# Expert tiles: transposition of bf16 halves by DMA in place of f32 transpositions on TensorE

## The chip, the cores and the metric

One core of one Trainium2 chip. The metric is the device time of one execution in microseconds.

## What is computed

A two-layer block on x of 32 x 256 x 256 (f32). Layer 0 is cross attention and then a mixture of experts; layer 1 is gated cross attention and then a quantized feed-forward network with a convolution. The change lies in the experts alone:

```
xf = layernorm(x).reshape(8192, 256)
scores = softmax(xf @ w_router.T);  weights, indices = top_k(scores, 2)
h = silu(xf @ w1[e]) * (xf @ w3[e])          # e = 0..7, hidden width 352
y = h @ w2[e]
out = sum over the two chosen experts of weight * y
```

The products are made as sums of bf16 products of high and low halves, three to each f32 product: high x high, high x low, low x high.

## The kernel before, in words

The program runs four stages in a row: `attention_first` (which also routes each token row to its expert's block of `sent_rows` in HBM), `experts`, `attention_second`, `ternary_ffn`. In the profiled execution `experts` lies at about 573 to 1050 us.

`experts` (line 1756) works on 71 tiles of 256 rows (NT = 2 blocks of 128 rows, D = 256 columns, KC = 2 chunks of 128 columns), each belonging to one expert. Every engine walks the list of tiles with its own instructions, written out; semaphores tie them together.

- SP: `load(b)` (L1860) brings a tile's rows into `xe`, one of four buffers, after the results of tile b - 4 were made (y1); `store(b)` (L1866) waits for y1 of tile b and sends `yo` to `back_rows`. The first four loads go out ahead; in the loop (L1876) each store is followed by the load of tile b + 4. SP also issues 13 loads of later stages' weights, one behind each of tiles 1 to 13 (`early`, L1882), and one 64 KB DMA `places` at tile 20 (L1885).
- TensorE: `turn_tile(b)` (L2088, matmul line L2080) waits for the load and makes four f32 transpositions of 128 x 128 into the PSUM tile `ps_t`. `up(b, c)` (L2094) makes, for each of three chunks c of the hidden width, 12 matmuls of 256 columns (w1 and w3, two chunks of D, three terms); `down(b)` (L2104) makes 18. Loop (L2117): up chunk 0 of tile b, turn_tile(b + 1), up chunks 1 and 2, then down(b - 1). The tiles 0 and 1 are turned ahead of the loop. Matmuls of up and down have line L2073.
- ScalarE: `rows_high` (L1913) copies `ps_t` into bf16, `xt_hi`; `silu` (L1918); `results` (L1923) makes `yo` from PSUM with the row's routing weight, in two activations that signal y0 and y1. Order in a tile: silu 0, rows_high(b + 1), silu 1, silu 2, results(b - 1) (L1933).
- VectorE: `rows_low` (L2003) makes `xt_lo` = `ps_t` - `xt_hi`; `hidden` (L2009) multiplies silu(w1 x) with w3 x into `h`. Some preparation of later weights lies between tiles (L2014).
- GpSimd: `h_lo`, the low half of `h` (L1898), which down needs.

Of the kernel before, what the change touches and what calls it, by code (L numbers as in the profile page):

```python
# [14 lines left out]
ALU = mybir.AluOpType  # L15
ACT = mybir.ActivationFunctionType
F32 = mybir.dt.float32
# [3 lines left out]
P = 128  # L21
# [1734 lines left out]
def experts(nc, sem, a, sh, pre, slots, sent, back_rows, places):  # L1756
# [7 lines left out]
    SLOTS = B * NT * 2  # L1764
    with ExitStack() as ctx:
# [8 lines left out]
        ident, bases, ends, tri, iota, starts, ones, seen = sh.ident, sh.bases, sh.ends, sh.tri, sh.iota, sh.starts, sh.ones, sh.seen  # L1774
# [23 lines left out]
        xe = sb("xe", [P, 4, NT, WIDE], F32)  # L1798
        xt_hi, xt_lo = sb("xt_hi", [P, 2, KC, N], BF16), sb("xt_lo", [P, 2, KC, N], BF16)
# [15 lines left out]
        ps_t = psum("ps_t", [P, 2, 512])  # L1815
# [10 lines left out]
        e_ld = [sem(f"e_e_ld{i}") for i in range(4)]  # L1826
# [3 lines left out]
        ue = Signal(sem("e_ue"), "xT")  # L1830
# [8 lines left out]
        once = Batch(0, 0, 0)  # L1839

# [7 lines left out]
        def _(sp):  # L1848
# [11 lines left out]
            def load(b):  # L1860
                at = sp.value_load(row[0:1, b.n:b.n + 1], min_val=0, max_val=E * ROOM + SPARE - ROWS)
                if b.n >= 4:
                    my.wait(sp, b.back(4), "y1")
                sp.dma_start(xe[:, b.n % 4, :, :], block_of(at)).then_inc(e_ld[b.n % 4], 16)
# [6 lines left out]
            for b in tiles[0:4]:  # L1871
                load(b)
            for par in range(2):
                sp.wait_ge(sh.s_slots[par], 16 * (B // 2))
            sp.dma_start(slot_i[:, :, :], slots.rearrange("b p k -> p b k")).then_inc(s_slot, 16)
            for b in tiles:  # L1876
                store(b)
                if b.n + 4 < TILES:
                    load(tiles[b.n + 4])
                if b.n == 0:  # L1880
                    sp.wait_ge(sh.s_low, 6)
                if 0 <= b.n - 1 < len(early):  # L1882
# [26 lines left out]
        def _(act):  # L1909
# [13 lines left out]
            def results(b):  # L1923
                md.wait(act, b, "down")
                if b.n >= 2:
                    act.wait_ge(o_st[b.par], 16 * (b.n // 2))
                for t in range(NT):
                    nc.scalar.activation(yo[:, b.par, t, :], ps_y[:, b.par, t * D:(t + 1) * D], ACT.Copy,  # L1928
                                         scale=xe[:, b.n % 4, t, D:D + 1]).then_inc(my.sem, 1)

            rows_high(tiles[0])
            rows_high(tiles[1])
# [18 lines left out]
        def _(dve):  # L1951
# [103 lines left out]
            rows_low(tiles[0])  # L2055
            rows_low(tiles[1])
            for b in tiles:
                for c, _at, k in CH:
                    hidden(b, c, k)
                    if c == 0 and 0 < b.n < TILES - 1:  # L2060
                        rows_low(tiles[b.n + 1])
# [7 lines left out]
        def _(pe):  # L2069
# [6 lines left out]
            def turn(to, rows_):  # L2076

                for c in range(KC):
                    for t in range(NT):
                        last = nc.tensor.transpose(to[:, c * N + t * P:c * N + (t + 1) * P], rows_[:, t, c * P:(c + 1) * P], ident[:, :])  # L2080
                return last

# [5 lines left out]
            def turn_tile(b):  # L2088
                pe.wait_ge(e_ld[b.n % 4], 16 * (b.n // 4 + 1))
                ua.wait(pe, b.back(2), "hi")  # L2090
                uv.wait(pe, b.back(2), "lo")
                turn(ps_t[:, b.par, :], xe[:, b.n % 4, :, :]).then_inc(ue.sem, 1)

            def up(b, c, at, k, e):  # L2094
                ua.wait(pe, b, "hi")
                uv.wait(pe, b, "lo")
                mh.wait(pe, b.back(1), f"h{c}")
                for i, (hi, lo) in enumerate((w1, w3)):
                    last = product(ps_ab[0:k, c, i * N:(i + 1) * N],
                                   [(w[:, kc, bass.ds(e, 1), at:at + k].rearrange("p o k -> p (o k)"), x[:, b.par, kc, :])  # L2100
                                    for kc in range(KC) for w, x in ((hi, xt_hi), (hi, xt_lo), (lo, xt_hi))])
# [12 lines left out]
            turn_tile(tiles[0])  # L2114
            turn_tile(tiles[1])
            before = None
            for b in tiles:  # L2117
                e = pe.value_load(owner[0:1, b.n:b.n + 1], min_val=0, max_val=E - 1)
                for c, at, k in CH:
                    up(b, c, at, k, e)  # L2120
                    if c == 0 and 0 < b.n < TILES - 1:
                        turn_tile(tiles[b.n + 1])
# [524 lines left out]
```

## Time and profile before

| what | value |
|---|---|
| runs | 1982.25, 1988.02, 1982.32 us; median 1982.32 |
| profiled execution | span 1987.6 us from the first to the last instruction; its own time isn't listed apart; of the three times only 1988.02 is as long as its span |
| TensorE | busy 1746.9 us (88%) |
| VectorE, ScalarE, GpSimd | 1466.4, 1418.6, 1006.9 us |
| expert stage | about 456 us between first loads in use and last down part |

In all views times are microseconds unless marked ns. PE is TensorE's matmuls, PEld its weight loads, DVE VectorE, ACT ScalarE, POOL GpSimd, SPq the issuing of DMAs by SyncE. A matmul's length is its time in the pipeline: of two in a row the starts are closer together than the length. The clock is the share of full speed that was granted to TensorE.

### The profile page before, as it was taken

The page shows a single profiled execution, that of the slowest core. Times are in us where ns is not written, and L with a number is a line of the kernel's source. Part 1 is how long each engine was busy: PE and PEld are TensorE (multiplying, and loading weights), DVE is VectorE, ACT ScalarE, POOL GpSimd, SP SyncE. Part 2 cuts the span into 40 slices and gives each one's busy share as a digit, 9 for nine tenths or more (in the row PEclk, how much of TensorE's full clock was granted, in tenths as well). Part 3 has the DMA queues.
Part 4 walks back from the last instruction along what each step waited for, and adds up shares of the span by engine and source line. Part 5 has one row for each costly group of instructions (what it writes and reads, how often), then busy time and mean ns, then how long its engine had stood idle before and what let it go on. Part 6 is the DMA issues. An engine that isn't in the chain of part 4 may idle for free. (4 is left out here: it accounts for less than half of the span.)

```text
span 1987.6 us, 52512 instructions
## 1 busy us (share of the span) xinstructions
PE 1746.9 (88%) x16125; PEld 1469.8 (74%) x16125; DVE 1466.4 (74%) x4269; ACT 1418.6 (71%) x2753; POOL 1006.9 (51%) x1295
## 2 busy tenths in 40 slices
PE   4889999999729999999993999999999578888887
PEld 3667878787519998999992788888888366666666
DVE  4889999999434343333332999999998599999996
ACT  5888999999424443444442777777777499999998
POOL 3557888887523233322226676676662133333332
PEclk8899999999859999999996999999999799999999
DMA  5434343433234352222224455545552112212111
GB/s 173 155 111 146 117 128 110 132 109 95 81 97 143 93 83 85 89 84 89 89 78 92 102 125 113 122 110 121 116 119 68 54 49 64 63 63 63 63 58 54
DMA packets 190557, 194.16 MB, mean 98 GB/s; under 512 B 33184, under 2 KB 180128, under 8 KB 189408
## 3 DMA queue, kind: packets, MB, share of 16 engines
q1 hardware_dynamic: 165856, 157.88, 26.7%
q0 software_dynamic: 24576, 34.62, 8.5%
q8 instruction: 78, 1.28, 0.3%
q14 instruction: 47, 0.39, 0.1%
HBM read 118.13 MB, written 74.30 MB: 97 GB/s over the span
## 5 line engine op out<-in xcount | busy, mean ns | idle before, releaser
L1898 POOL TENSOR_TENSOR e_h_lo<-e_h 128x256 bf16<-128x256 f32 (+1 forms) x213 | 138.7, 652 | 334.3 <-DVE e_h L2012 334.3
L2012 DVE TENSOR_TENSOR e_h<-e_s,e_ps_ab 128x256 f32<-128x256 f32 (+1 forms) x213 | 89.3, 420 | 275.2 <-ACT e_s L1921 275.2
L2073 PE MATMUL e_ps_ab<-e_xt_hi,k_w_hi 128*128 128x256 bf16 (+1 forms) x852 | 233.3, 274 | 0.0
L2073 PE MATMUL e_ps_ab<-e_xt_hi,k_w_lo 128*128 128x256 bf16 (+1 forms) x852 | 233.0, 273 | 0.0
L2073 PE MATMUL e_ps_ab<-e_xt_lo,k_w_hi 128*128 128x256 bf16 (+1 forms) x852 | 233.0, 273 | 0.0
L1921 ACT ACTIVATE e_s<-e_ps_ab 128x256 f32<-128x256 f32 (+1 forms) x213 | 81.5, 383 | 148.3 <-PE e_ps_ab L2073 148.2
L2473 PE MATMUL f_ps_h<-f_qh,p_arena 128*128 128x256 bf16 x512 | 123.8, 281 | 35.1 <-DVE f_ql L2437 28.5
L1928 ACT ACTIVATE e_yo<-e_ps_y,e_xe 128x256 f32<-128x256 f32 x142 | 59.6, 471 | 112.7 <-PE e_ps_y L2073 112.7
L2473 PE MATMUL f_ps_h<-f_ql,p_arena 128*128 128x256 bf16 x512 | 122.9, 279 | 0.0
L2073 PE MATMUL e_ps_y<-e_w_hi,e_h 128*128 (+1 forms) x426 | 116.5, 273 | 0.0
L2073 PE MATMUL e_ps_y<-e_w_hi,e_h_lo 128*128 (+1 forms) x426 | 115.9, 272 | 0.0
L2073 PE MATMUL e_ps_y<-e_w_lo,e_h 128*128 (+1 forms) x426 | 115.7, 272 | 0.0
L1289 POOL DMA_INDIRECT a_xa<-back_rows,a_where x64 | 107.7, 1683 | 15.7 <-issue 15.2
L2251 POOL TENSOR_TENSOR f_y<-f_y,f_tmp 128x510 f32<-128x510 f32 x32 | 43.6, 1362 | 136.6 <-DVE f_y L2372 136.6
L1299 POOL DMA_INDIRECT a_xa<-back_rows,a_where x64 | 100.6, 1572 | 21.4 <-issue 21.0
L2473 PEld LDWEIGHTS f_ps_h<-f_qh,p_arena 128*128 128x128 bf16 x512 | 50.9, 99 | 61.1 <-DVE f_ql L2437 36.3
L2073 PEld LDWEIGHTS e_ps_ab<-e_xt_hi,k_w_hi 128*128 (+1 forms) x852 | 90.6, 106 | 7.2 <-issue 0.4
L2073 PEld LDWEIGHTS e_ps_ab<-e_xt_hi,k_w_lo 128*128 (+1 forms) x852 | 90.7, 106 | 7.1
L2073 PEld LDWEIGHTS e_ps_ab<-e_xt_lo,k_w_hi 128*128 (+1 forms) x852 | 90.9, 107 | 6.8
L499 POOL DMA_INDIRECT sent_rows<-k_xn,k_slot x64 | 71.2, 1112 | 18.5 <-issue 18.5
L462 POOL DMA_INDIRECT sent_rows<-k_xn,k_slot x64 | 64.0, 1001 | 17.4 <-issue 17.4
L506 POOL TENSOR_TENSOR a_qf<-p_arena 128x512 f32<-128x512 f32 x32 | 40.7, 1273 | 63.3 <-DVE p_arena L674 63.3
(433 smaller groups left out, 6621.5 us busy)
## 6 DMA issues: line engine op xcount, KB each, us to landing
e_xe<-sent_rows SPq DMA_DIRECT2D x71, 272.0 KB, 2.8
back_rows<-e_yo SPq DMA_DIRECT2D x71, 256.0 KB, 2.1
x_rows<-a_x SPq DMA_DIRECT2D x64, 256.0 KB, 2.7
p_arena<-in_xT SPq DMA_DIRECT2D x32, 256.0 KB, 4.7
a_xa<-in_x SPq DMA_DIRECT2D x32, 256.0 KB, 4.8
a_xr<-in_x SPq DMA_DIRECT2D x32, 256.0 KB, 4.6
a_xa<-x_rows SPq DMA_DIRECT2D x32, 256.0 KB, 3.3
x_rows<-a_xa SPq DMA_DIRECT2D x32, 256.0 KB, 2.2
```

The source lines that it names most:

```text
L462: nc.gpsimd.indirect_dma_start(sent[:, :], bass.IndirectOffsetOnAxis(ap=slot[:, b.par, t, 0:1], axis=0), e_xn[:, b.par, t, :], None).then_ ...
L499: nc.gpsimd.indirect_dma_start(sent[:, :], bass.IndirectOffsetOnAxis(ap=slot[:, b.par, t, 1:2], axis=0), e_xn[:, b.par, t, :], None).then_ ...
L506: nc.gpsimd.tensor_tensor(qf[:, :, :], rc[:, :, :], rs[:, :, :], ALU.add).then_inc(gp0.sem, 1)
L1289: nc.gpsimd.indirect_dma_start(xa[:, b.par, t, :], None, y_rows[:, :], bass.IndirectOffsetOnAxis(ap=where[:, b.par, 2 * t + 1:2 * t + 2], ...
L1299: nc.gpsimd.indirect_dma_start(xa[:, b.par, t, :], None, y_rows[:, :], bass.IndirectOffsetOnAxis(ap=where[:, b.par, 2 * t + 0:2 * t + 1], ...
L1898: nc.gpsimd.tensor_tensor(h_lo[0:k, b.par, c, :], h[0:k, b.par, c, :], h_hi[0:k, b.par, c, :], ALU.subtract).then_inc(mg.sem, 1)
L1921: nc.scalar.activation(s[0:k, c, :], ps_ab[0:k, c, 0:N], ACT.Silu).then_inc(ma.sem, 1)
L1928: nc.scalar.activation(yo[:, b.par, t, :], ps_y[:, b.par, t * D:(t + 1) * D], ACT.Copy, scale=xe[:, b.n % 4, t, D:D + 1]).then_inc(my.sem, 1)
L2012: nc.vector.tensor_tensor(h[0:k, b.par, c, :], s[0:k, c, :], ps_ab[0:k, c, N:2 * N], ALU.mult).then_inc(mh.sem, 1)
L2073: last = nc.tensor.matmul(to, left, right, start=(i == 0), stop=(i == len(terms) - 1))
L2251: nc.gpsimd.tensor_tensor(y[:, 2:4, 0:N - 1], y[:, 2:4, 0:N - 1], tmp[:, 2:4, 0:N - 1], ALU.add).then_inc(gp4.sem, 1)
L2473: last = nc.tensor.matmul(dst, l, r, start=(n == 0), stop=(n == len(terms) - 1))
```

## The change

The rows of a tile are split into halves in their own layout (rows on partitions), straight from `xe`: two activations for the high half (`rows_[..., 0, ...]`) and two subtractions for the low one, one for each block of 128 rows. SP then issues two DMA transpositions a tile, `turn(b)`, the high halves' as soon as they are made, the low ones' after theirs, each of 128 partitions x 512 bf16 elements (128 KB) into one of three buffers `turned`. TensorE's transpositions, their PSUM tile and their signal are gone; up waits for both DMAs. The halves are made three tiles ahead instead of one, and `xe` has six buffers instead of four, so that the first six loads go out ahead. In SP's loop turn(b + 3) stands between store(b) and load(b + 6).

```diff
+    XE, XT = 6, 3
-        xe = sb("xe", [P, 4, NT, WIDE], F32)
-        xt_hi, xt_lo = sb("xt_hi", [P, 2, KC, N], BF16), sb("xt_lo", [P, 2, KC, N], BF16)
+        xe = sb("xe", [P, XE, NT, WIDE], F32)
+        rows_ = sb("rows", [P, 2, 2, KC, NT, P], BF16)
+        turned = sb("turned", [P, XT, 2, KC, N], BF16)
-        ps_t = psum("ps_t", [P, 2, 512])
+        def turned_away(eng, b):
+            if b is not None:
+                eng.wait_ge(t_ld[b.n % XT], 32 * (b.n // XT + 1))
             def load(b):
-                if b.n >= 4:
-                    my.wait(sp, b.back(4), "y1")
+                if b.n >= XE:
+                    my.wait(sp, b.back(XE), "y1")
+            def turn(b):
+                ua.wait(sp, b, "hi")
+                me.wait(sp, b.back(XT), "up2")
+                for part in range(2):
+                    if part:
+                        uv.wait(sp, b, "lo")
+                    nc.sync.dma_start_transpose(turned[:, b.n % XT, part, :, :].rearrange("p k (t n) -> p (k t) n", t=NT),
+                                                rows_[:, b.par, part, :, :, :].rearrange("p k t n -> p (k t n)")).then_inc(t_ld[b.n % XT], 16)
-            for b in tiles[0:4]:
+            for b in tiles[0:XE]:
                 load(b)
+            for b in tiles[0:XT]:
+                turn(b)
             for b in tiles:
                 store(b)
-                if b.n + 4 < TILES:
-                    load(tiles[b.n + 4])
+                if b.n + XT < TILES:
+                    turn(tiles[b.n + XT])
+                if b.n + XE < TILES:
+                    load(tiles[b.n + XE])
             def rows_high(b):
-                ue.wait(act, b, "xT")
-                me.wait(act, b.back(2), "up2")
-                nc.scalar.activation(xt_hi[:, b.par, :, :].rearrange("p k n -> p (k n)"), ps_t[:, b.par, :], ACT.Copy).then_inc(ua.sem, 1)
+                act.wait_ge(e_ld[b.n % XE], 16 * (b.n // XE + 1))
+                turned_away(act, b.back(2))
+                for t in range(NT):
+                    last = nc.scalar.activation(rows_[:, b.par, 0, :, t, :], xe[:, b.n % XE, t, 0:D].rearrange("p (k n) -> p k n", k=KC), ACT.Copy)
+                last.then_inc(ua.sem, 1)
-                    if c == 0 and 0 < b.n < TILES - 1:
-                        rows_high(tiles[b.n + 1])
+                    if c == 0 and b.n + 3 < TILES:
+                        rows_high(tiles[b.n + 3])
             def rows_low(b):
                 ua.wait(dve, b, "hi")
-                me.wait(dve, b.back(2), "up2")
-                nc.vector.tensor_tensor(xt_lo[:, b.par, :, :].rearrange("p k n -> p (k n)"), ps_t[:, b.par, :],
-                                        xt_hi[:, b.par, :, :].rearrange("p k n -> p (k n)"), ALU.subtract).then_inc(uv.sem, 1)
+                for t in range(NT):
+                    last = nc.vector.tensor_tensor(rows_[:, b.par, 1, :, t, :], xe[:, b.n % XE, t, 0:D].rearrange("p (k n) -> p k n", k=KC),
+                                                   rows_[:, b.par, 0, :, t, :], ALU.subtract)
+                last.then_inc(uv.sem, 1)
-            def turn_tile(b):
-                pe.wait_ge(e_ld[b.n % 4], 16 * (b.n // 4 + 1))
-                ua.wait(pe, b.back(2), "hi")
-                uv.wait(pe, b.back(2), "lo")
-                turn(ps_t[:, b.par, :], xe[:, b.n % 4, :, :]).then_inc(ue.sem, 1)
             def up(b, c, at, k, e):
-                ua.wait(pe, b, "hi")
-                uv.wait(pe, b, "lo")
+                turned_away(pe, b)
...
-            turn_tile(tiles[0])
-            turn_tile(tiles[1])
-                    if c == 0 and 0 < b.n < TILES - 1:
-                        turn_tile(tiles[b.n + 1])
```

VectorE makes rows_low(b + 3) where it made rows_low(b + 1), and both engines make the first three tiles' halves ahead of the loop.

## Rows read from the trace of the kernel before

**Rows 1.** The page: span and busy time of each engine

```profile
span 1987.6 us, 52512 instructions
...
PE 1746.9 (88%) x16125; PEld 1469.8 (74%) x16125; DVE 1466.4 (74%) x4269; ACT 1418.6 (71%) x2753; POOL 1006.9 (51%) x1295
```

**Rows 2.** Busy time by stretch: expert stage, two up parts; busy (x instructions), clock, DMA, GB/s

```profile
590.00:1046.00 456.00, 452.41 (x4114) 415.66 (x4114) 157.91 (x306) 187.49 (x430) 139.85 (x217) 0.99 0.33 92
1032.17:1036.54 4.37, 4.37 (x43) 4.09 (x40) 1.53 (x3) 2.21 (x5) 0.81 (x2) 1.00 0.17 60
1038.51:1042.44 3.93, 3.93 (x38) 3.65 (x36) 0.84 (x2) 1.61 (x4) 0.80 (x2) 1.00 0.21 71
```

**Rows 3.** Timeline of one tile: start, length, engine, line, what, idle before it

```profile
801.96 0.27 PE L2073 MATMUL e_ps_y<-e_w_hi,e_h 128*128 x1
...
803.07 1.53 POOL L1898 TENSOR_TENSOR e_h_lo<-e_h 96x256 bf16<-96x256 f32 x1 [0.69 <-DVE e_h L2012]
...
803.93 0.27 PE L2073 MATMUL e_ps_ab<-e_xt_hi,k_w_hi 128*128 128x256 bf16 x1
...
804.13 0.84 ACT L1928 ACTIVATE e_yo<-e_ps_y,e_xe 128x256 f32<-128x256 f32 x2 [1.59 <-PE e_ps_y L2073]
...
805.00 0.36 SPq L1868 DMA_DIRECT2D back_rows<-e_yo  x1
...
805.24 0.60 PE L2080 MATMUL e_ps_t<-k_ident,e_xe 128*128 128x128 f32 x4
805.44 0.38 ACT L1921 ACTIVATE e_s<-e_ps_ab 128x256 f32<-128x256 f32 x1 [0.47 <-PE e_ps_ab L2073]
...
805.68 0.27 PE L2073 MATMUL e_ps_ab<-e_xt_hi,k_w_hi 128*128 128x256 bf16 x1
...
806.10 0.38 SPq L1864 DMA_DIRECT2D e_xe<-sent_rows  x1
...
808.30 0.27 PE L2073 MATMUL e_ps_y<-e_w_hi,e_h 128*128 x1
```

**Rows 4.** Waits of SP's queue, 590 to 1040 us: total, times, longest

```profile
SPq L1868 <- ACT e_yo L1928: 327.7, 68, 14.5
```

**Rows 5.** Groups of instructions, 600 to 1040 us: busy, mean ns, idle before

```profile
L2012 DVE TENSOR_TENSOR e_h<-e_s,e_ps_ab 128x256 f32<-128x256 f32 (+1 forms) x206 | 86.4, 420 | 265.4 <-ACT e_s L1921 265.4
L1921 ACT ACTIVATE e_s<-e_ps_ab 128x256 f32<-128x256 f32 (+1 forms) x206 | 78.8, 383 | 141.6 <-PE e_ps_ab L2073 141.6
...
L2006 DVE TENSOR_TENSOR e_xt_lo<-e_ps_t,e_xt_hi 128x512 bf16<-128x512 f32 x69 | 47.7, 691 | 18.5 <-ACT e_xt_hi L1916 18.3
L1916 ACT ACTIVATE e_xt_hi<-e_ps_t 128x512 bf16<-128x512 f32 x69 | 41.2, 597 | 6.8 <-PE e_ps_t L2080 3.3
```

**Rows 6.** DMA issues of the whole run: count, KB each, us to landing

```profile
e_xe<-sent_rows SPq DMA_DIRECT2D x71, 272.0 KB, 2.8
back_rows<-e_yo SPq DMA_DIRECT2D x71, 256.0 KB, 2.1
...
k_w_f<-in_fw SPq DMA_DIRECT2D x2, 1024.0 KB, 5.3
...
k_ident<-in_ident SPq DMA_DIRECT2D x1, 64.0 KB, 2.5
...
e_slot_i<-slots SPq DMA_DIRECT2D x1, 64.0 KB, 5.3
...
places<-e_placed SPq DMA_DIRECT2D x1, 64.0 KB, 13.3
```

**Rows 7.** Timeline of the stage's start

```profile
586.16 3.83 SPq L1864 DMA_DIRECT2D e_xe<-sent_rows  x4
...
591.73 0.39 PE L2073 MATMUL e_ps_ab<-e_xt_hi,k_w_hi 128*128 128x256 bf16 x1
```

**Rows 8.** Timeline around the places transfer

```profile
733.39 0.47 SPq L1887 DMA_DIRECT2D places<-e_placed  x1
...
747.99 0.66 PE L2080 MATMUL e_ps_t<-k_ident,e_xe 128*128 128x128 f32 x4 [3.05 <-DMA e_xe<-sent_rows]
```

More of the change, by code:

```diff
@@ L1772, in experts @@
         I32 = mybir.dt.int32
-        ident, bases, ends, tri, iota, starts, ones, seen = sh.ident, sh.bases, sh.ends, sh.tri, sh.iota, sh.starts, sh.ones, sh.seen
+        bases, ends, tri, iota, starts, ones, seen = sh.bases, sh.ends, sh.tri, sh.iota, sh.starts, sh.ones, sh.seen
         zeros, w1, w3 = sh.zeros, sh.w1, sh.w3
@@ L1823, in experts @@
         s_count = sem("e_count")
-        e_ld = [sem(f"e_e_ld{i}") for i in range(4)]
+        e_ld = [sem(f"e_e_ld{i}") for i in range(XE)]
+        t_ld = [sem(f"e_t_ld{i}") for i in range(XT)]
         o_st = [sem(f"e_o_st{i}") for i in range(2)]
@@ L1829, in experts @@
         uv = Signal(sem("e_uv"), "lo")
-        ue = Signal(sem("e_ue"), "xT")
         me = Signal(sem("e_me"), "up0 up1 up2")
@@ L1861, in load @@
                 at = sp.value_load(row[0:1, b.n:b.n + 1], min_val=0, max_val=E * ROOM + SPARE - ROWS)
-                if b.n >= 4:
-                    my.wait(sp, b.back(4), "y1")
-                sp.dma_start(xe[:, b.n % 4, :, :], block_of(at)).then_inc(e_ld[b.n % 4], 16)
+                if b.n >= XE:
+                    my.wait(sp, b.back(XE), "y1")
+                sp.dma_start(xe[:, b.n % XE, :, :], block_of(at)).then_inc(e_ld[b.n % XE], 16)
+            def turn(b):
[6 more added lines that the diff above has]
+                                                rows_[:, b.par, part, :, :, :].rearrange("p k t n -> p (k t n)")).then_inc(t_ld[b.n % XT], 16)
             def store(b):
@@ L1928, in results @@
                     nc.scalar.activation(yo[:, b.par, t, :], ps_y[:, b.par, t * D:(t + 1) * D], ACT.Copy,
-                                         scale=xe[:, b.n % 4, t, D:D + 1]).then_inc(my.sem, 1)
-            rows_high(tiles[0])
-            rows_high(tiles[1])
+                                         scale=xe[:, b.n % XE, t, D:D + 1]).then_inc(my.sem, 1)
+            for b in tiles[0:3]:
+                rows_high(b)
             for b in tiles:
@@ L2053, in prepare @@
                     nc.vector.tensor_scalar(pre.half_tg[:, :], pre.tg[:, 2:3], 0.5, None, ALU.mult).then_inc(wv, 1)
-            rows_low(tiles[0])
-            rows_low(tiles[1])
+            for b in tiles[0:3]:
+                rows_low(b)
             for b in tiles:
@@ L2059, in _ @@
                     hidden(b, c, k)
-                    if c == 0 and 0 < b.n < TILES - 1:
-                        rows_low(tiles[b.n + 1])
+                    if c == 0 and b.n + 3 < TILES:
+                        rows_low(tiles[b.n + 3])
                 if b.n == 4:
@@ L2074, in product @@
                 return last
[L2076 to L2081, printed above, removed]
             nc.tensor.matmul(ps_y[:, 1, 0:E], ones[:, :], seen[:, :], start=True, stop=True).then_inc(s_count, 1)
@@ L2099, in up @@
                     last = product(ps_ab[0:k, c, i * N:(i + 1) * N],
-                                   [(w[:, kc, bass.ds(e, 1), at:at + k].rearrange("p o k -> p (o k)"), x[:, b.par, kc, :])
-                                    for kc in range(KC) for w, x in ((hi, xt_hi), (hi, xt_lo), (lo, xt_hi))])
+                                   [(w[:, kc, bass.ds(e, 1), at:at + k].rearrange("p o k -> p (o k)"), turned[:, b.n % XT, part, kc, :])
+                                    for kc in range(KC) for w, part in ((hi, 0), (hi, 1), (lo, 0))])
                 last.then_inc(me.sem, 1)
@@ L2120, in _ @@
                     up(b, c, at, k, e)
-                    if c == 0 and 0 < b.n < TILES - 1:
-                        turn_tile(tiles[b.n + 1])
                 if b.n == 1:
```

## The prediction

> **What bounds the kernel now.** I read the page's busy shares, then the stretches, one tile's timeline, SP's waits, and the DMA issues. The busy shares say little: TensorE has 88% of the span, the others half to three quarters [rows 1]. The expert stage from 590 to 1046 us says more: TensorE is busy 452.4 of 456.0 us at a granted clock of 0.99, the upper of its two levels (2.4 GHz), while VectorE, ScalarE and GpSimd have 158, 187 and 140 [rows 2]. Here TensorE's own stream is the bound, and what leaves it shortens the stage as long as nothing else comes late.
>
> The price of the transpositions is read from a natural control. Tile 69's up part contains the last turn_tile and takes 4.37 us up to the down part behind it; tile 70's contains none and takes 3.93 [rows 2]. The difference, 0.44, is also the distance from 805.24 (four transpositions) to 805.68 (the next matmul) in a tile from the middle. The down parts of two tiles begin at 801.96 and 808.30, so the period is 6.34 us [rows 3], and without transpositions P = 5.90.
>
> Then see when SP acts. A down part ends where the next up part begins, 803.93; ScalarE's two result activations run 804.13 to 804.97 and the store is issued 805.00 to 805.36 [rows 3]. SP waits for just that, 327.7 us in 68 waits [rows 4].
>
> **The change, part by part.**
>
> *Removed from TensorE.* 69 turn_tiles inside the loop (the first two stand in the start): at most 69 x 0.44 = **-30.4 us**, if nothing takes the place.
>
> *The halves.* ScalarE's one activation of 597 ns becomes two of 256 elements, for which I take the silu's 383: 0.77. VectorE's 691 ns becomes two, at the 420 of the product h: 0.84 [rows 5]. Both engines idle over half the stage, so 0.17 and 0.15 more a tile cost nothing by themselves. VectorE now reads both operands from SBUF; an h_lo of GpSimd that overlapped other SBUF work of VectorE took 1.53 us, and yet ended at 804.60 for a down part beginning at 808.30 [rows 3]: 3.7 us of cover, and TensorE's wait for lo2 if that were gone.
>
> *The wait that is added.* The rows in halves have two buffers, so rows_high(b + 3) first waits until both transpositions of tile b + 1 have landed. On ScalarE it stands right behind silu 0 of tile b, and behind it are queued silu 1, silu 2 and results(b - 1). GpSimd and VectorE wait for the silus; SP waits for the results, because the store of b - 1 stands ahead of the turn of b + 2. So there is a closed loop that advances one tile a round:
>
> turn(b + 1) landed, rows_high(b + 3) 0.77, silu 1 and silu 2 with their issue gaps 0.80, results(b - 1) with its gap 0.86, issue of store(b - 1) 0.39, then turn(b + 2), which lands L later.
>
> Durations are 383 ns a silu [rows 5], 0.84 for the pair of results and 0.36 for the store [rows 3], plus 0.02 to 0.03 between neighbours. Nothing in it overlaps: **the period can't be under L + 2.82**. The old one returns at L = 3.52; below L = 3.08 TensorE's 5.90 rules and the whole gain is kept. In between, VectorE's rows_low(b + 3) stands ahead of h1 and adds a short wait of TensorE's second chunk, but no time to the loop.
>
> (The looser condition, that the pair is there when up begins, has 5.90 - 1.43 = 4.47 us, the 1.43 being the end of the store's issue after up's begin. It would let L = 4.4 pass; the wait on ScalarE is the tighter one.)
>
> *L, from the first issue to the second landing.* No transposing DMA is in this trace. As plain transfers: the second is issued 0.38 us after the first [rows 3] and lands in 2.8 like the load or 2.1 like the store [rows 6]; 1024 KB take 5.3 and 272 KB 2.8, 0.30 MB a microsecond, so the first's 128 KB ahead of it are 0.43. That is L = 2.9 to 3.6, the lower bound. From the other side: 64 KB in 4096 runs of 16 bytes land in 5.3 us and 64 KB in rows of 512 bytes in 2.5 [rows 6], so 4096 short reads cost 2.8; a transposition made in that many runs gives L = 3.2 + 2 x 2.8 = 8.8 (short writes into HBM, 13.3 us for 64 KB, would be further still, but neither side is HBM here). I take the load's 3.6 and add what 512 runs cost at that rate, 0.35, for each: a block of 128 columns is 256 bytes in a partition, four blocks in 128 partitions. **L = 4.3**, near the plain end because most of what a transfer costs here is landing, not bytes. Period 4.3 + 2.82 = 7.12, and 67 rounds of 0.78 more than now: **+52 us** in place of the -30.
>
> The Trainium skill has two rules for what no row here shows, and they disagree. "Advanced Engine Details and Errata", X-Bar Transpose (TRN2), says that transposing DMAs are as fast as ordinary ones; by it L is the 2.9 to 3.6 of the plain rows, and the sum is between the whole gain and no change. "VectorE: DVE Perf Modes", The three transpose paths, gives 1309 ns for one 128 x 128 bf16 block by DMA against 390 ns on TensorE; an estimate by that page, eight blocks a tile in sequence, is 10.5 us for the pair and a stage some 470 us longer.
>
> *The load behind.* load(b + 6) goes out after two more DMAs and is wanted by rows_high(b + 6), three tiles later less 3.9 us: some 9 us of cover for a landing of 2.8. It costs nothing.
>
> *The start.* Four loads take 3.83 us from 586.16, and up begins at 591.73 [rows 7]. Six take until 591.9, the halves of tile 0 are ready by then, and the pair lands 4.3 - 0.4 later, the low half not being waited for: about 595.8, **+4 us**.
>
> *The places transfer.* It is issued at 733.39 and lands 13.3 us later; TensorE now waits 3.05 us for a load behind it [rows 6, 8]. That load will be early, but a turn is issued 7 us behind places and lands some 3.5 us later than else, with no slack in the loop: **+0.5**. The 13 early loads stand behind each load(b + 6) and are mostly gone when the next store comes; the 1024 KB ones take 5.3 us and may not be: **+1**.
>
> Sum: 52 + 4 + 0.5 + 1 = **+58 us**. Against the profiled 1987.6 that is 2045; the median, 1982.3, is 5.3 us below that span, and as no term here explains the spread I add to the median: **2040 us**.
>
> **The rivals.**
>
> A. *Faster.* The pair lands as plain stores do: L = 0.38 + 2.1 + 0.43 = 2.9, under 3.08. The stage is TensorE's again with 5.90 a tile: 1982.3 - 30.4 + 3.6 - 3 (places gone), 1953, with part of the early loads' delays 1956. For: both ends are SBUF, and the store, which reads from it, is the quicker of the rows. Against: the store just issued is 256 KB in the same queue ahead of them. Chance 0.14.
>
> B. *In between*, L = 3.1 to 3.6, periods of 5.92 to 6.42: 1958 to 1993. For: the plain end with the load's landing is 3.6. Chance 0.11, half of it no change.
>
> C. *The issue is dear.* SP spends 1 to 2 us on each transposition instead of 0.38, or the data are at half the small-run rate: L = 5.2 to 6.5, 2102 to 2190; at L = 5.8, 2143. For: such a transfer has to be cut into many more pieces than a copy of the same bytes. Against: nothing in the trace prices an issue above 0.47 unless it had to wait. Chance 0.25.
>
> D. *Small runs in full*, L = 8.8, period 11.6: 67 x 5.3 = +354, 2344. The slot table speaks for it, the SBUF ends against. Chance 0.06.
>
> E. *The edit saves nothing and costs nothing*: the transpositions leave TensorE but its matmuls wait for h1 (VectorE's rows_low ahead of it) by the same 0.44. That needs L near 3.5, so it is within B. With a TensorE idle for 1.2 us a tile the granted clock might fall to its lower level as well, which at most doubles 5.90, a period of 11.8 and a time like D's; no row shows this stage with such gaps. 0.02.
>
> **How the numbers follow.** The forecast with L = 3.6 to 5.2 has 0.42, its own range is 1993 to 2102. Over 0.3%, about 6 us, is what a measurement of this kernel can tell from none. Slower: 0.42 + 0.25 + 0.06 + 0.02 = 0.75; same 0.05; faster 0.14 + 0.06 = 0.20. For 8 in 10 the range keeps all cases from A to most of C: 1955 to 2170.
>
> **What would show it.** Right: ScalarE waits at rows_high for the transposition, every tile, and not for the matmuls; period = L + 2.8, with L measured from the first issue to the second landing; TensorE idle over 1 us a tile before its first up matmul, the L2080 group gone. A hidden pair would show up parts 3.93 us long, a period of 5.90 and SP waiting for results at the old distance. If the period is L + 2.8 but L is not 4.3, only the size was wrong, and the lengths of SP's issues say whether C is it. If TensorE waits while L + 2.8 is under the period, the loop is not the cause and my mechanism falls.

## The result and the profile after

The changed kernel takes 2032.4 us in the median (2025.2 to 2036.0, 4 runs) against 1983.6 (1982.3 to 1988.0, 4 runs) before: a ratio of 1.0237, 95% interval 1.022 to 1.0254, so 49 us slower. The forecast was 2040.

The page and the busy time by stretch of the changed kernel, to be held against [rows 1, 2]:

```profile
span 2034.0 us, 52155 instructions
...
PE 1725.7 (85%) x15841; PEld 1427.1 (70%) x15841; DVE 1459.0 (72%) x4340; ACT 1397.3 (69%) x2824; POOL 1001.1 (49%) x1295
...
DMA packets 267804, 212.76 MB, mean 105 GB/s; under 512 B 110432, under 2 KB 257376, under 8 KB 266656
```

```profile
590.00:1092.00 502.00, 438.59 (x3818) 376.63 (x3819) 149.44 (x373) 165.19 (x495) 137.54 (x217) 0.98 0.54 118
```

284 matmuls have gone from TensorE, and the expert stage has grown from 456 to 502 us all the same: TensorE is now idle 63 us of it, where it was idle 4. Measured in both traces between the same two marks, from the matmul of the token counts (line 2083 before) to SP's first load of `places` in the next stage, the stage takes 477.8 us before and 531.9 after: +54.1. That stage explains the whole difference; the rest of the two executions differs by -7.7 us, in the stages that the change doesn't touch. In what follows "the stage" is this length. It comes from the one profiled execution of each kernel. It can be compared between chips, because most of what differs between chips lies outside it: outside the stage the profiled executions, with the same code, take 1517 to 1522 us on the chip where the kernel before takes 1995.7, and 1505 to 1509 on the one where it takes 1985.8. But the executions of one kernel differ by 2 to 15 us, so differences of some 5 us between two stages are not shown by one execution each.

The waits of the changed kernel, 600 to 1080 us (who waited, for whom: total, times, longest):

```profile
DVE e_rows L2027 <- ACT e_rows L1936: 319.2, 66, 10.3
ACT e_rows L1936 <- DMA e_turned<-e_rows: 314.9, 66, 12.0
...
PE e_ps_ab L2095 <- DMA e_turned<-e_rows: 35.8, 28, 7.5
PE e_ps_ab L2095 <- DVE e_h L2034: 26.9, 62, 0.6
```

The large one is not TensorE's. ScalarE stands at rows_high (L1936) for 315 us, almost 5 us a tile, waiting for a transposition to land; TensorE's own waits for the turned tile are a tenth of that. Two rounds of the loop, in the timeline of ScalarE and SP, against [rows 3]:

```profile
800.77 0.72 ACT L1936 ACTIVATE e_rows<-e_xe 128x256 bf16<-128x256 f32 x2 [5.67 <-DMA e_turned<-e_rows]
801.40 0.63 ACT L1942 ACTIVATE e_s<-e_ps_ab 128x256 f32<-128x256 f32 x2
...
801.93 0.82 ACT L1949 ACTIVATE e_yo<-e_ps_y,e_xe 128x256 f32<-128x256 f32 x2
...
802.78 0.36 SPq L1883 DMA_DIRECT2D back_rows<-e_yo  x1
...
803.24 2.55 SPq L1878 DMA_TRANSPOSE e_turned<-e_rows  x2
...
807.10 0.72 ACT L1936 ACTIVATE e_rows<-e_xe 128x256 bf16<-128x256 f32 x2 [4.07 <-DMA e_turned<-e_rows]
807.72 0.63 ACT L1942 ACTIVATE e_s<-e_ps_ab 128x256 f32<-128x256 f32 x2
...
808.25 0.82 ACT L1949 ACTIVATE e_yo<-e_ps_y,e_xe 128x256 f32<-128x256 f32 x2
...
809.10 0.36 SPq L1883 DMA_DIRECT2D back_rows<-e_yo  x1
...
809.56 3.23 SPq L1878 DMA_TRANSPOSE e_turned<-e_rows  x2
...
814.43 0.72 ACT L1936 ACTIVATE e_rows<-e_xe 128x256 bf16<-128x256 f32 x2 [5.06 <-DMA e_turned<-e_rows]
```

Read it downwards: the landing releases rows_high at 807.10, the two silus that were queued behind follow at 807.72, the results at 808.25, the store is issued when they end, at 809.10, and the next turn at 809.56. Every line starts when the one before allows it. L, from the first issue to the second landing, is read here up to the start of the rows_high that the landing releases (0.1 us after the landing itself): 3.86 us in the first round and 4.87 in the second. From there to the next turn it is 2.46 to 2.5 us in 61 of 66 rounds; in the other five SP is later, by up to 1.2 us.

The DMA rows that answer to [rows 6], the whole run's plain transfers first, then the transpositions' issue on SP (min/median/max in ns) and their landing:

```profile
e_xe<-sent_rows SPq DMA_DIRECT2D x71, 272.0 KB, 2.8
back_rows<-e_yo SPq DMA_DIRECT2D x71, 256.0 KB, 2.3
```

```profile
L1878 SPq DMA_TRANSPOSE e_turned<-e_rows x142: 1207/1260/2602, 585.6 to 1083.5; - x142
...
DMA to landing us min/median/max: 2.4/2.5/10.4
```

One transposition is issued in 1.26 us and lands 2.5 after its issue began; 1.27 + 2.5 is the 3.8 of an undisturbed pair. Over 66 rounds L is 4.1 in the median and 4.6 in the mean, in two heaps, 3.82 to 4.3 and 4.6 to 5.8, and two single rounds of 7.4 (behind a load of 1024 KB) and 10.85 (behind the places transfer).

### The profile page after: what moved, and what is told of

Read it like the earlier page. It is cut to its first block and busy times, and to the rows that moved or that the text cites. A ratio compares the mean times of both kernels' runs of the same rounds, so it can differ in the third digit from the quotient of the medians.

```text
span 2034.0 us, 52155 instructions
## 1 busy us (share of the span) xinstructions
PE 1725.7 (85%) x15841; PEld 1427.1 (70%) x15841; DVE 1459.0 (72%) x4340; ACT 1397.3 (69%) x2824; POOL 1001.1 (49%) x1295
## 5 line engine op out<-in xcount | busy, mean ns | idle before, releaser
L2095 PE MATMUL e_ps_ab<-e_turned,k_w_hi 128*128 128x256 bf16 (+1 forms) x1704 | 292.0, 276 | 87.0 <-DMA e_turned<-e_rows 59.8
L2027 DVE TENSOR_TENSOR e_rows<-e_xe,e_rows 128x256 bf16<-128x256 f32 x142 | 54.4, 424 | 331.1 <-ACT e_rows L1936 331.1
L1936 ACT ACTIVATE e_rows<-e_xe 128x256 bf16<-128x256 f32 x142 | 51.3, 408 | 332.5 <-DMA e_turned<-e_rows 320.9
L2095 PEld LDWEIGHTS e_ps_ab<-e_turned,k_w_hi 128*128 (+1 forms) x1704 | 170.4, 107 | 127.3 <-issue 113.5
L2095 PE MATMUL e_ps_ab<-e_turned,k_w_lo 128*128 128x256 bf16 (+1 forms) x852 | 234.6, 275 | 0.0
L2034 DVE TENSOR_TENSOR e_h<-e_s,e_ps_ab 128x256 f32<-128x256 f32 (+1 forms) x213 | 82.8, 415 | 30.5 <-ACT e_s L1942 25.4
L2095 PEld LDWEIGHTS e_ps_ab<-e_turned,k_w_lo 128*128 (+1 forms) x852 | 91.3, 107 | 7.5
L1942 ACT ACTIVATE e_s<-e_ps_ab 128x256 f32<-128x256 f32 (+1 forms) x213 | 72.6, 372 | 14.1 <-PE e_ps_ab L2095 14.0
L889 PE MATMUL a_ps_b<-a_wo,a_ot 128*128 128x256 f32 x256 | 64.6, 398 | 0.6 <-ACT a_ot L578 0.6
```

The costliest lines, as they stand in the source:

```text
L889: last = nc.tensor.matmul(dst, l, r, start=(n == 0), stop=(n == len(terms) - 1))
L1942: nc.scalar.activation(s[0:k, c, :], ps_ab[0:k, c, 0:N], ACT.Silu).then_inc(ma.sem, 1)
L2027: last = nc.vector.tensor_tensor(rows_[:, b.par, 1, :, t, :], xe[:, b.n % XE, t, 0:D].rearrange("p (k n) -> p k n", k=KC), rows_[:, b.par, ...
L2034: nc.vector.tensor_tensor(h[0:k, b.par, c, :], s[0:k, c, :], ps_ab[0:k, c, N:2 * N], ALU.mult).then_inc(mh.sem, 1)
L2095: last = nc.tensor.matmul(to, left, right, start=(i == 0), stop=(i == len(terms) - 1))
```

## The experiments

All kernels are the changed one with the edit shown. Times are given beside those of the kernel before on the same chip, as ratios with their 95% interval, since the chips differ by up to 12 us; tile periods are taken from store to store, the first 68 (the last two tiles drain the stage).

| kernel | stage us | period, median / mean | ratio to before |
|---|---|---|---|
| before | 477.8 | 6.34 / 6.39 | 1 |
| changed | 531.9 | 6.64 / 7.11 | 1.0237 (1.022 to 1.0254) |
| four buffers of halves | 479.8 | 5.91 / 6.36 | 1.0022 (1.0007 to 1.0036) |
| halves behind the results | 474.4 | 5.91 / 6.29 | 1.0036 (1.0018 to 1.0054) |
| turn ahead of the store | 452.4 | 5.90 / 5.97 | 0.9893 (0.9868 to 0.9918) |
| a third transposition | 599.5 | 7.89 / 8.10 | 1.0635 (1.0611 to 1.0658) |
| one transposition | 468.0 | 5.90 / 6.19 | 0.9966 (0.995 to 0.9981) |
| plain copies | 468.6 | 5.90 / 6.20 | 0.9982 (0.9968 to 0.9996) |
| both halves in one DMA | 477.1 | 5.91 / 6.31 | 1.0019 (1.0005 to 1.0034) |
| more instructions on GpSimd | 529.4 | 6.69 / 7.08 | 1.0258 (1.0235 to 1.028) |
| a third of the matmuls | 491.9 | 6.36 / 6.62 | 1.0082 (1.006 to 1.0104) |
| deep version | 447.9 | 5.90 / 5.83 | 0.9868 (0.9849 to 0.9887) |

**Is it the loop? Cut it at three places, and lengthen it.** First, more buffers of halves, picked by b.n % 4 wherever b.par picked one of two:

```diff
-        rows_ = sb("rows", [P, 2, 2, KC, NT, P], BF16)
+        rows_ = sb("rows", [P, 4, 2, KC, NT, P], BF16)
-                turned_away(act, b.back(2))
+                turned_away(act, b.back(4))
```

> The changed kernel with four buffers of row halves instead of two, so that rows_high(b + 3) waits for the transpositions of tile b - 1 and not of b + 1; nothing else differs. Theory (closed loop through ScalarE: landed turn, rows_high, two silus, results, store's issue, next turn, whose period in the changed kernel is L + 2.46 with L = 4.63 in the mean): the loop is cut, the next condition is that the pair is there when up begins, (5.90 + 1.43 + L)/2 = 5.6 at the usual L of 3.86 and 6.0 at the mean, so TensorE is nearly the bound again with 5.9 to 6.0 us a tile; ScalarE no longer waits for transpositions; 1955 to 1965 us. Rival (TensorE waits because two transpositions, an issue of 2.5 us and a landing of 2.5, are simply too long for one tile, or load the DMA queue beside loads and stores): the buffers change nothing, 7.0 us a tile and 2025 to 2035 us.

ScalarE's wait for transpositions is gone and the median tile takes 5.91 us, as the loop's theory says and its rival excludes. But the time missed the expectation, by 35 us as it stands and by some 24 when this slower chip is allowed for: it is that of the kernel before. The mean period is 6.36, not 5.9 to 6.0. One error was to put the mean of L into a condition that only the long rounds break: a short L brings nothing below 5.90, a long one costs all that it has over the margin, and the round behind places alone costs 8.4 us (14.28). The other was the half in (5.90 + 1.43 + L)/2. The rows of a tile whose up waited for its pair, in this kernel:

```profile
845.99 0.38 PE L2095 MATMUL e_ps_ab<-e_turned,k_w_hi 128*128 128x256 bf16 x2
...
847.52 4.11 SPq L1878 DMA_TRANSPOSE e_turned<-e_rows  x2
...
853.07 0.39 PE L2095 MATMUL e_ps_ab<-e_turned,k_w_hi 128*128 128x256 bf16 x2 [1.01 <-DMA e_turned<-e_rows]
```

The turn for the next tile is issued 1.53 us after an up begins, it lands L = 5.42 later, and the next up begins 0.13 behind that. So there is a second loop, through TensorE, results and store, of L + 1.66 a round. 25 of the 29 tiles whose up waited for the landing have this to 0.1 us. It too has slope one; it is only the shorter of the two.

The second cut, in ScalarE's order; rows_low moves in the same way behind VectorE's three products of the loop:

```diff
                     silu(b, c, k)
-                    if c == 0 and b.n + 3 < TILES:
-                        rows_high(tiles[b.n + 3])
                 if b.n:
                     results(tiles[b.n - 1])
+                if b.n + 3 < TILES:
+                    rows_high(tiles[b.n + 3])
```

> The changed kernel with rows_high(b + 3) behind results(b - 1) on ScalarE instead of behind silu 0, and rows_low(b + 3) behind the last product on VectorE; two buffers, SP as in the changed kernel. A third place at which the loop can be cut: the wait for the landed transposition no longer stands ahead of silu 1, silu 2 and the results. Theory (closed loop through ScalarE's order): most tiles take 5.90 us; what is left is the second condition, up's begin, (7.33 + L)/2, that only rounds with a long L break, as with four buffers of halves, so the stage (count matmul to next stage) is 475 to 485 us and the time within 10 us of the kernel before. Rival (it isn't the queue behind the wait but the two buffers as such that cost): the stage stays over 520 us.

474.4 us, within 6 us of the other cut and 57 under the changed kernel. The execution that was profiled is the fastest of this kernel's ten, 6 us under their median, so the two cuts are equal as far as this shows. The time is 5 us over the kernel before, as expected. Two buffers are enough; what cost was the queue behind the wait.

The third cut, on SP:

```diff
-                store(b)
                 if b.n + XT < TILES:
                     turn(tiles[b.n + XT])
+                store(b)
```

> The changed kernel with two buffers of halves, but on SP turn(b + 3) ahead of store(b) instead of behind it; nothing else differs. Theory (closed loop through results and store): the loop is opened at another place, since the turn waits only for its halves and for up2 of tile b, 2.9 us or more before the store; the halves still wait for the landing on ScalarE, but that landing is now early. 5.90 us a tile, 1953 to 1960 us. Rival one (too long a transfer): 2025 to 2035 us as before. Rival two (the wait on ScalarE is a cost by itself, whatever SP does): ScalarE still waits 4 to 5 us a tile and the time stays over 2010 us.

This alone turns the change into a gain of 1.1% (23 us on this chip); the expectation, held against the first chip's time before, was 24 to 30. The timeline of this kernel shows the pair issued 4 us and more before the store that it used to wait for, and rows_high following silu 0 with no wait:

```profile
799.55 2.52 SPq L1878 DMA_TRANSPOSE e_turned<-e_rows  x2
...
803.82 0.37 SPq L1883 DMA_DIRECT2D back_rows<-e_yo  x1
804.26 0.38 ACT L1942 ACTIVATE e_s<-e_ps_ab 128x256 f32<-128x256 f32 x1 [0.47 <-PE e_ps_ab L2095]
804.54 0.71 ACT L1936 ACTIVATE e_rows<-e_xe 128x256 bf16<-128x256 f32 x2
```

It also tells what kept the first two cuts from a gain. They still had long rounds, each of which cost what it was over: with four buffers of halves the 68 periods have 31 us in all above 5.90. Here the pair is issued early enough to cover nearly all of those, and 4 us are left above 5.90.

Then the loop made longer by one known piece, the low halves turned a second time into a buffer that nothing reads:

```diff
+                nc.sync.dma_start_transpose(again[:, b.n % XT, :, :].rearrange("p k (t n) -> p (k t) n", t=NT),
+                                            rows_[:, b.par, 1, :, :, :].rearrange("p k t n -> p (k t n)")).then_inc(t_ld[b.n % XT], 16)
...
-                eng.wait_ge(t_ld[b.n % XT], 32 * (b.n // XT + 1))
+                eng.wait_ge(t_ld[b.n % XT], 48 * (b.n // XT + 1))
```

> The changed kernel with a third transposition a tile: the low halves are transposed once more into a buffer that nobody reads, and up and rows_high wait for it too. It adds one issue of 1.26 us and so 1.26 us to L, nothing on any engine. Theory (closed loop, slope one): 67 rounds x 1.26 = +84 us against the changed kernel, 2110 to 2125 us, 8.3 us a tile. Rival (the looser condition, that the pair is there when up begins, with slope one half): +42 us, 2070 to 2080 us. If DMA throughput were the bound, more than slope one: over 2140 us.

The ratio is 4.0 points above that of the changed kernel, 79 us on 1984; the stage is 68 us longer, where 84 were expected of the time. The absolute 2121 lies in the expectation's window, but this chip is 12 us slower. One round with its third issue:

```profile
881.10 2.54 SPq L1879 DMA_TRANSPOSE e_turned<-e_rows  x2
883.68 1.27 SPq L1881 DMA_TRANSPOSE e_again<-e_rows  x1
...
886.30 0.72 ACT L1939 ACTIVATE e_rows<-e_xe 128x256 bf16<-128x256 f32 x2 [4.47 <-DMA e_again<-e_rows]
...
888.78 2.54 SPq L1879 DMA_TRANSPOSE e_turned<-e_rows  x2
```

Short rounds have L = 5.16 and last 7.63 us, against 3.86 and 6.32: +1.30 in, +1.31 out. Over all rounds the mean of L rises by 1.03, from 4.63 to 5.66, and that of the period by 0.99: the slope is one, and the rise is less than 1.26 because the long rounds grew less. The slope alone doesn't tell this loop from the looser condition, as the expectation had it, since the loop through TensorE found above has slope one as well. The level does: by L + 1.66, with L up to the landing, short rounds would last 5.90 (TensorE's own time) in the changed kernel and 6.7 here, and they last 6.32 and 7.63, in both L + 2.46. The loop is shown, then, from both sides.

**What does turning cost?** One transposition alone, of the high halves; the products take those in place of the low ones, so this kernel doesn't compute the right result. As up no longer waits for the low halves, ScalarE gets a wait for those of tile b + 1 ahead of rows_high(b + 3), which is not in the cut below:

```diff
-                eng.wait_ge(t_ld[b.n % XT], 32 * (b.n // XT + 1))
+                eng.wait_ge(t_ld[b.n % XT], 16 * (b.n // XT + 1))
...
-                for part in range(2):
+                for part in range(1):
...
-                                    for kc in range(KC) for w, part in ((hi, 0), (hi, 1), (lo, 0))])
+                                    for kc in range(KC) for w, part in ((hi, 0), (hi, 0), (lo, 0))])
```

> The changed kernel with the high halves' transposition alone; the low ones are still computed on VectorE but not transposed, and the products high weights x low rows use the high rows in their place, so the number of matmuls is the same. L falls from 3.86 to 2.5 us. Theory (closed loop, L + 2.46): 4.96 us is under TensorE's 5.90, so the whole gain comes back: 5.90 us a tile, 1953 to 1962 us, and TensorE hardly waits. Rival (transpositions on the DMA rings cost by their number or hold up loads and stores): half of the loss stays, about 2005 us.

The median tile is at 5.90 and no more, but the gain over the kernel before is 0.3%, not over 1%. So the expectation failed. Short rounds have L = 2.5, and 2.5 + 2.46 is well under 5.90; some rounds have 4.1 to 4.3, 6.6 to 6.8 us with the loop, and the round behind places takes 13.5. Again the long rounds.

Plain copies in the same places:

```diff
-                    nc.sync.dma_start_transpose(turned[:, b.n % XT, part, :, :].rearrange("p k (t n) -> p (k t) n", t=NT),
-                                                rows_[:, b.par, part, :, :, :].rearrange("p k t n -> p (k t n)")).then_inc(t_ld[b.n % XT], 16)
+                    nc.sync.dma_start(turned[:, b.n % XT, part, :, :].rearrange("p k n -> p (k n)"),
+                                      rows_[:, b.par, part, :, :, :].rearrange("p k t n -> p (k t n)")).then_inc(t_ld[b.n % XT], 16)
```

> The changed kernel with both transpositions replaced by plain copies of the same 128 KB within SBUF, so that the products are made of rows that aren't turned; queue, order, waits and number of DMAs are the same. It prices turning against copying. Theory (closed loop, period L + 2.46 with L the time from the first issue to the second landing): a plain copy is issued in 0.38 us where a transposition took 1.26, and if it lands 2.1 to 2.5 us later, L is 2.5 to 2.9 and the loop 5.0 to 5.4, under TensorE's 5.90: 5.90 us a tile and about 28 us under the kernel before. The second thing that it tells apart: in the changed kernel L is 3.86 in half of the rounds and 4.2 to 5.8 in the others, and in the ones looked at the long rounds were those with a packet of the instruction queue in them. If that is a matter of turning, a copy shows no rounds with L over 3.5; if any pair of DMAs is held up by an instruction fetch, its long rounds stay, by 1 to 2 us.

The copy's L is 2.73 where the transpositions have 3.86; the rows for its issue (ns) and landing:

```profile
L1878 SPq DMA_DIRECT2D e_turned<-e_rows x142: 465/599/2237, 596.6 to 1030.8; - x142
...
DMA to landing us min/median/max: 2.0/2.1/9.0
```

Turning costs 1.13 us on the pair, and 63 us in the stage, through the loop: it is under TensorE's 5.90 with the short L of a copy and over it with that of a transposition. The rule of the Trainium skill, "Advanced Engine Details and Errata", X-Bar Transpose (TRN2), that these DMAs are as fast as ordinary ones, doesn't hold here for transfers of 128 KB; they move the same bytes but take 1.26 us on the issuing engine instead of 0.60, and land after 2.5 us instead of 2.1. The expectation's second part went the other way than "a matter of turning": copies have long rounds as well, 4.1 to 4.7 us. The first part failed too: a copy is issued in 0.60 us, not 0.38, and the kernel wins 3 us over before, not 28.

Both halves in one DMA of twice the size:

```diff
-                ua.wait(sp, b, "hi")
+                uv.wait(sp, b, "lo")
                 me.wait(sp, b.back(XT), "up2")
-                for part in range(2):
-                    if part:
-                        uv.wait(sp, b, "lo")
-                    nc.sync.dma_start_transpose(turned[:, b.n % XT, part, :, :].rearrange("p k (t n) -> p (k t) n", t=NT),
-                                                rows_[:, b.par, part, :, :, :].rearrange("p k t n -> p (k t n)")).then_inc(t_ld[b.n % XT], 16)
+                nc.sync.dma_start_transpose(turned[:, b.n % XT, :, :, :].rearrange("p a k (t n) -> p (a k t) n", t=NT),
+                                            rows_[:, b.par, :, :, :, :].rearrange("p a k t n -> p (a k t n)")).then_inc(t_ld[b.n % XT], 16)
```

> The changed kernel with one transposition a tile of 128 x 1024 elements, high and low halves together, once the low ones are made. The same blocks are turned, with one issue and one landing. If a transposition is priced by its blocks (1.26 us of issue for four), the issue is 2.4 to 2.6 us, the landing still 1.2 us after its end, L = 3.8 and the time that of the changed kernel within 10 us. If it is priced by instruction, the issue is 1.3 to 1.5 us, L = 2.6, the loop 5.1 us, under TensorE's 5.90, and the time 10 to 25 us under the kernel before. The theory of the loop holds in either case: period = L + 2.46, if that is over 5.90.

```profile
L1875 SPq DMA_TRANSPOSE e_turned<-e_rows x71: 1232/1313/3221, 594.5 to 1035.0; - x71
...
DMA to landing us min/median/max: 3.1/3.1/9.8
```

Eight blocks are issued in 1.31 us, four in 1.26: the issue is, nearly, a price per instruction. The landing grows by 0.6 us for four more blocks, so L falls to 3.17 and not to 2.6, the loop to 5.6, the median tile to 5.91, and the stage by 55 us. The time is 0.2% over the kernel before and not 10 to 25 us under it; the mean period is 6.31, because of the long rounds once more. Beginning the high halves early, the idea of the split into two, costs more than it gives: the low halves are ready anyhow when SP comes to the turn, which is still issued 2.46 us after rows_high begins. The Trainium skill, "VectorE: DVE Perf Modes", The three transpose paths, gives 1309 ns for one block; that isn't borne out as a price per block either, since an estimate by it for eight is 10.5 us, and they landed after 3.1.

**What makes rounds long?** In the changed kernel, each round's stretch between issue and landing was searched for packets of the instruction queues. 29 rounds with a packet on the first of them (q8, 16 KB each) have L = 5.39 in the mean, 37 without have 4.04; with plain copies 22 have 4.09 and 44 have 2.76 (the 2.92 in the expectations is too high). The number of hits says nothing: the stretches are two thirds of the time, so 26 of the 40 packets would fall into them by chance. The moment of the packet does. Leaving out the two single rounds, all 26 rounds with L over 4.5 contain a packet, and it begins 1.3 to 3.6 us behind the first issue. The two packets that begin later still, just ahead of the landing, go with L = 3.9, the two more than 1.1 us ahead of the issue with 3.9 and 4.0, and seven that begin 0.6 to 0.3 us ahead of it with 4.1 to 4.3. A packet takes about 1.05 us. Without the two single rounds, the means are 5.20 and 3.94. To see whether that is cause or sign, instructions were added:

```diff
+                for j in range(64):
+                    nc.gpsimd.memset(junk[0:1, 64 * b.n + j:64 * b.n + j + 1], 0.0)
```

> The changed kernel with 64 stores of two bytes more a tile on GpSimd, behind its three h_lo, to a scratch tile that nobody reads. GpSimd is idle 5.5 us a tile there, and needs some 2 to 3 for them. It tests whether instruction fetches lengthen L: in the changed kernel the 29 rounds in which the instruction queue moved a packet had L = 5.39 in the mean and the other 37 had 4.04, and plain copies show the same, 4.09 against 2.92. 64 instructions of 64 bytes are 4 KB a tile, one more packet of 16 KB in every fourth tile, 17 in all. Theory (fetches hold up the transpositions, and the loop passes it on): more packets on the instruction queue, 15 more long rounds of 1.35 us, the stage 15 to 25 us longer, 550 us. Rival (the fetches are only a sign of something else that comes every second tile): the stage stays within 5 us of the changed kernel's 531.9. If GpSimd itself becomes late, TensorE's waits for h_lo would show it.

The queues of this kernel, 590 to 1090 us (packets, MB, share of 16 engines); the changed kernel has 40 and 19 on the last two:

```profile
q1 hardware_dynamic: 123946, 58.96, 54.4%
q8 instruction: 40, 0.66, 0.6%
q14 instruction: 54, 0.44, 0.3%
```

35 more packets, but of 8 KB and on the other instruction queue, and the stage got no longer: the expectation failed. Of the rounds without a 16 KB packet, those with one of 8 KB have L = 4.08 and the others 3.94. So these fetches don't hold up the transpositions to speak of. What was left was TensorE's, and those were made fewer:

```diff
-                                    for kc in range(KC) for w, part in ((hi, 0), (hi, 1), (lo, 0))])
+                                    for kc in range(KC) for w, part in ((hi, 0),)])
...
-                                    for c, _at, k in CH for hh, w in ((h_hi, w2[0]), (h_hi, w2[1]), (h_lo, w2[0]))])
+                                    for c, _at, k in CH for hh, w in ((h_hi, w2[0]),)])
```

> The changed kernel with one of the three matmuls of each product left out twice: up and down keep high x high alone (18 matmuls a tile for 54), everything else is the same, waits, halves, both transpositions, loads and stores. TensorE isn't in the loop, so its 3.9 us less a tile don't shorten it. What changes is the number of instructions that TensorE needs to fetch: the stage's 40 packets of 16 KB on the first instruction queue should be some 15. The 35 packets of 8 KB that the stores on GpSimd had added went over the other instruction queue and changed nothing, so what is left of the fetch theory is: TensorE's 16 KB packets hold up the DMAs. Theory: 25 packets fewer, 18 to 20 of 29 long rounds become short ones, 1.35 us each: the stage 500 to 510 us instead of 531.9, mean L 4.2 to 4.3, and rounds with a packet still have L = 5.4. Rival one (packets are only a sign): mean L stays 4.6 and the stage over 525 us. Rival two (TensorE is in the loop after all, through h1): the stage falls under 480 us.

```profile
q8 instruction: 17, 0.28, 0.2%
q14 instruction: 19, 0.16, 0.1%
```

17 packets instead of 40, and 11 rounds with one in them instead of 29, with L = 5.03; the other 55 have 4.02, as before. The mean period falls from 7.11 to 6.62. The stage is 491.9, 8 us under the window of the expectation; some of that isn't the loop's, because the first and last tiles wait for TensorE (first store 33.6 instead of 37.4 us after the counts, last two periods 3.5 us less in all). This is the reading in which all of it agrees: a 16 KB packet for TensorE's instructions delays a pair of DMAs by about 1.0 to 1.35 us, and the loop has no slack for it. That the one changes with the other is shown; how the packet does it is not. This kernel has less of everything that TensorE does, so another effect of its work that comes in step with the fetches isn't excluded. The kernel shows one thing more, in its busy time by stretch:

```profile
600.00:1050.00 450.00, 273.77 (x1225) 172.84 (x1222) 143.50 (x358) 156.62 (x478) 132.10 (x208) 0.58 0.54 129
```

With a third of the matmuls and a granted clock of 0.58 (1.2 GHz would be 0.5) the round is 6.3 us as before. TensorE is not in the loop.

**A version that beats both.** Turn ahead of the store, four buffers of halves as in the first cut, halves made four tiles ahead, four buffers of turned rows and eight of loads, and three loads before the first turn:

```diff
-    XE, XT = 6, 3
+    XE, XT = 8, 4
...
-            for b in tiles[0:XE]:
+            for b in tiles[0:3]:
...
+                load(tiles[b.n + 3])
+            load(tiles[7])
```

> A version that should beat both: turn ahead of the store on SP, four buffers of halves, four of turned rows and eight of loads, all made four tiles ahead, and at the start three loads, then turns and loads in turn. Against turn-first alone (452.4 us from the count matmul to the next stage) it should save the wait of about 4 us behind the places transfer, since there are 5.9 us more of cover, and 3 us at the start, where six loads no longer stand ahead of the first turn. 5.90 us a tile throughout; 28 to 32 us under the kernel before, ratio 0.984 to 0.986. If the DMA queue is the limit, some tiles stay over 5.90.

27 us under the kernel before, ratio 0.9868, just short of the expectation. The first up begins 20.6 us after the counts instead of 24.0, 3.4 us earlier, as expected. The stage is 4.5 us shorter than with turn-first alone, where about 7 were expected, and the intervals of the two ratios overlap, so that this version beats that one isn't shown by the times. From up to up a tile takes 5.90 us in the mean; from store to store it is 5.83, because the first stores are late, behind the turns on SP. From 600 to 1010 us TensorE is busy 408.0 of 410.0:

```profile
600.00:1010.00 410.00, 407.98 (x3732) 373.54 (x3730) 175.89 (x367) 183.62 (x488) 137.90 (x213) 1.00 0.68 145
```

## Why the prediction was right, and where only by luck

- *The transpositions are worth 0.44 us a tile*, -30.4 in all if nothing takes their place: right. Wherever the loop is cut, tiles take 5.90 us.
- *The added wait closes a loop through ScalarE, results and store, which sets the period*: right, shown by three cuts and by the third transposition, with rounds of L + 2.46 in both kernels. It was the step that decided the sign; the condition that one sees first, that the pair must be there when up begins, would have let L = 3.86 pass, and predicted a gain.
- *2.82 us besides L*: 2.46 measured. The two activations of a pair and the silus start before their predecessors end (0.72, 0.53 and 0.85 from start to start), which the sum of lengths didn't see.
- *L = 4.3*: 4.1 in the median, 4.6 in the mean. The sum 7.12 against a mean of 7.11 is luck, an agreement of errors that cancel: 0.36 too much besides L, 0.3 too little in it. In L itself the terms were off too. I put the issue at 0.38 us and the landing at 3.9 with its additions; it is 1.26 and 2.5. The case with the dear issue, C, was right in kind and too high in size. The runs of 256 bytes are real: packets under 512 bytes rise by 77248, 544 for each of 142 transpositions, and by the trace's sizes these are the 512 of 256 bytes that had been counted and 32 of 4 bytes.
- *+52 for the loop*: mis-sized. The mean of 7.11 contains the rounds behind places and behind the first early load, which the prediction counts apart. Without them it is 6.96, against 6.34 before: 0.62 a round, 41 us in 66 rounds. The 11 us too many here are made up for by some 7 too few in the terms for places and the early loads; that the closing sum is near is luck in this part.
- *Spread of L*: absent from the prediction. It is what the first two cuts and the lighter transfers stumbled on.
- *The start, +4*: +4.8 (first up 24.0 us after the counts, 19.1 before).
- *The places transfer, +0.5*: mis-sized. The round behind it takes 14.26 us, 7.9 over a short one, where the old stall cost 3.3: +4.7. The turn behind places had L = 10.85, and the store ahead of it took 1.30 us to issue.
- *Early loads, +1*: the first of 1024 KB alone makes a round of 9.84 us, +3.5.
- *VectorE's halves ahead of h1 cost TensorE a wait but the loop nothing*: right, 26.9 us of such waits in 62 pieces, none of which lengthens a round.
- *TensorE idle over 1 us a tile before its first up matmul*, named as a sign: not so. It waits for the pair in 28 rounds only, 35.8 us; in the short rounds the pair is there in time, and the slack of 0.42 us is spent waiting for h1.
- *The clock might fall*, in rival E: it did not, the stage has 0.98, the upper level, with TensorE idle 63 of 502 us.
- The closing sum for the stage: 58 forecast, 54.1 measured; for the whole time 58 forecast, 49 measured.

## What to carry to other kernels

When a change adds a wait, write down what is queued behind it on that engine and follow those instructions until they return to the wait; if they do, the period is the sum around the ring, however much slack each part seems to have by itself. When that ring is cut, look for the next one: here it was L + 1.66, and the long rounds still broke it. Put producers of the next tile ahead of the consumers of an old one on a queue that issues both: moving one line on SP took 79 us off this stage. And test a margin against the long rounds of a transfer, not against its median: only lateness adds up.

## What the runs showed of the hardware

A transposing DMA within SBUF costs the issuing engine 1.26 us for 128 x 512 bf16 elements and 1.31 for 128 x 1024, where a plain copy of 128 KB costs 0.60; it lands 2.5 and 3.1 us after its issue begins, the copy after 2.1. For 128 KB it moves 512 packets of 256 bytes and 32 of 4 bytes. Beside TensorE's instruction packets of 16 KB, pairs of DMAs, turning or plain, took about 1.0 to 1.35 us longer in the mean (5.39 against 4.04, 4.09 against 2.76, 5.03 against 4.02); beside 8 KB packets for GpSimd's instructions it was 0.14 (4.08 against 3.94).
